# Where a decoder layer's projections wait: banks borrowed from the turned probabilities, self slots rearranged, loads moved

## The chip, the cores and the metric

The kernel runs on one core of one Trainium2 chip. The metric is the device time of the program in microseconds (us), lower is better. A core has TensorE (PE), VectorE (DVE), ScalarE (ACT), GpSimd (POOL) and SyncE (SP), each with its own instruction queue that is worked through in order, and 16 DMA engines shared by all queues. Engines wait for each other by semaphores.

## The reference, cut to what matters

A post-norm decoder layer over x of 8 batches x 256 tokens x 512, with 16 heads of 32:

```python
def _L0_attn_ref(x, Wq, Wk, Wv, Wo):        # 16 query heads, 4 key/value heads
    q = (x @ Wq) ...; k = (x @ Wk) ...; v = (x @ Wv) ...
    att = jnp.where(causal, q @ k.T * scale, -inf)
    return (softmax(att) @ v) @ Wo
def _L0_xattn_ref(q, latent_kv, Wq, Wkv_expand, Wout):   # keys and values from ctx_512 (256 x 128)
    ...causal softmax(q @ Wq.T, latent_kv @ Wkv_expand.T)... @ Wout.T
x = _layernorm(x + _L0_attn_ref(x, ...))
x = _layernorm(x + _L0_xattn_ref(x, ctx_512, ...))
x = _layernorm(x + _L0_ffn_ref(x, ...))      # gates, two levels of entanglement + paths, layer norms
```

Everything is float32. The kernel makes each float32 product from three products of a high and a low part, so an operand is first split: `hi` (a copy into the narrower format, ScalarE) and `lo` (the rest, VectorE or GpSimd).

## The kernel before, in words

**Turns, steps, slots.** The attention phase is a sequence of 17 turns (`Turn`): 8 self turns (one batch each), 8 cross turns, and a flush. `first` is the first, `selfs` a loop of two turns run three times, `last_self` the eighth; then `first_cross`, six `crosses`, `last_cross`, `flush`. A turn has four steps, one for each group of four heads. A step i works in three units: unit 0 is the first 128 queries of four heads, units 1 and 2 the other 128 queries of two heads each. In step i TensorE makes the scores of group i, unit by unit (`scores`, L1225, banks 0 to 2), and between them turns the probabilities of group i-1 (`transposes`, L1237), and behind unit 0 the outputs of group i-2 (`outputs`, L1257 and L1261). After each step stands a slot: projections that fill TensorE while the others work on the scores. The function `fillers` is the list, written by hand: `sk`, `sq`, `sv` are key, query and value projections of self attention, `ck`, `cq`, `cv` of cross attention, `wo` and `wout` the output projections of the turn before, `x1t` transposes of the normed x1, `fu` units of a product of two FFN weights, added up in `acc` (the tensor xb in the profile), `sp` and `gs` splits of FFN weights. Here sk, sq0, sq1 in a turn are for the next batch.

**Banks.** A projection is written to bank 3 or 4 in turn (`P_BANKS`, class `Products`), and waits (`wait_free`) until the product two before it has been drained. The turned probabilities go to banks 5 and 6 in turn (`T_BANKS`), 7 holds the outputs. Three units a step on two banks: unit u of step i has bank (3(i-1)+u) mod 2 of the two.

**Who drains.** ScalarE: exponentials of the step (L920), copies of turned units 0 (self) or 0 and 1 (cross) into probT (L933), then in the slot `hi` of the projections (L855) and copies of sv and cv (L859). VectorE: the maxima (L1049), reciprocals, outputs (L1066, L1070), copies of the other turned units (L1056), then in the slot `lo` (L969), the adds of fused units (L1013), `row_bias` (L998), and for wo the add to xres, statistics, and `normalise` (L1099), which waits for rstd from GpSimd (L769, L771). GpSimd splits outputs (`split_output`), x (`split_x`), FFN rows (L777) and makes path products (`path`, `path_bias`). SP issues all DMAs in order, with its waits between them: `stack` writes a split q or k into three rows (L586, L600), `store` waits for its own store to land, `load_piece` loads a piece of the cross weights, `load_row` FFN rows.

**The cross weights.** They come as pieces of 512 columns, six of them parked in zone_raw. `split_at` says in which slot ScalarE (L847) and VectorE (L961) split them: in `last_self` piece 0 in slot 0, 1 and 2 in slot 1, 3 and 4 ahead of slot 2, 5 ahead of slot 3.

## Time and profile before

| | |
|---|---|
| median of 3 runs | 988.41 us (985.12 to 989.49) |
| the profiled execution: its time, its span | 984.96 us, 983.1 us |
| mean granted clock of TensorE | 0.971 of full speed |
| TensorE matmuls, weight loads | 892.4 us (91%), 735.8 us (75%) |
| VectorE, ScalarE, GpSimd | 677.2 (69%), 550.1 (56%), 496.7 us (51%) |

The attention phase ends near 650 us; behind it stands the FFN phase, which the diff leaves alone. Busy time of matmuls is modelled and they are pipelined; a stretch in which TensorE waits is marked in the timeline as idle, with the engine that ended it. The granted clock is the share of full speed that TensorE was given; its two levels are 1.0 and 0.5 (2.4 and 1.2 GHz), a value between them is a mixture over the stretch.

### The profile page before, as it was taken

How to read it: one execution, taken by the hardware profiler on the slowest of the kernel's cores; microseconds unless marked ns; L12 is line 12 of the kernel's file. 1: busy time of each engine (PE TensorE's matmuls, PEld its weight loads, DVE VectorE, ACT ScalarE, POOL GpSimd, SP SyncE). 2: the span in 40 equal slices, each digit the busy share in tenths (PEclk: the TensorE clock that was granted, in tenths of full speed). 3: DMA queues.
4: the chain of work that ended last, by engine and by line, in shares of the span. 5: the costliest groups of instructions: out<-in, count | busy, mean ns of one | idle time of the engine just before them, and what ended most of it. 6: DMA issues, size and time to landing. Idle time of an engine off the chain costs nothing. (4 is left out here: it accounts for less than half of the span.)

```text
span 983.1 us, 19518 instructions
## 1 busy us (share of the span) xinstructions
PE 892.4 (91%) x5892; PEld 735.8 (75%) x5892; DVE 677.2 (69%) x2055; ACT 550.1 (56%) x1674; POOL 496.7 (51%) x793
## 2 busy tenths in 40 slices
PE   4999999998898899999999998669899999999893
PEld 4888888887776678778777877457678778778672
DVE  4687778786785777777876766426757657667557
ACT  4756556664664566565755556427564464564461
POOL 0445555455755345454645432610665565566466
PEclk9999999999899999999999999879999999999997
DMA  4644243444665556574654636344002001001001
GB/s 155 222 144 158 98 160 128 160 160 143 210 205 145 168 159 194 166 225 121 188 170 138 181 110 197 132 167 155 0 1 85 3 1 55 32 1 40 4 0 43
DMA packets 79075, 118.53 MB, mean 121 GB/s; under 512 B 7920, under 2 KB 41744, under 8 KB 78224
## 3 DMA queue, kind: packets, MB, share of 16 engines
q1 hardware_dynamic: 78992, 117.52, 37.2%
q8 instruction: 40, 0.66, 0.3%
q14 instruction: 43, 0.35, 0.1%
HBM read 58.76 MB, written 17.83 MB: 78 GB/s over the span
## 5 line engine op out<-in xcount | busy, mean ns | idle before, releaser
L920 ACT ACTIVATE prob<-bank,nmax 128x128 f32<-128x128 f32 (+1 forms) x512 | 209.9, 431 | 38.5 <-DVE nmax L1049 36.9
L161 PE MATMUL bank<-w_ffn,hT 128*128 128x512 f32 x768 | 192.8, 402 | 0.0
L1049 DVE CUSTOM_DVE_ANT_0 bank<-bank,mask 128x128 f32<-128x128 f32 (+1 forms) x512 | 167.6, 383 | 4.0 <-PE bank L1225 3.7
L161 PEld LDWEIGHTS bank<-w_ffn,hT 128*128 128x128 f32 x768 | 141.5, 189 | 30.9
L161 PE MATMUL bank<-xT,w_att 128*128 128x256 f32 x864 | 124.1, 298 | 22.0 <-DVE w_att L961 10.3
L161 PEld LDWEIGHTS bank<-xT,w_att 128*128 128x128 f32 x864 | 115.4, 201 | 31.7 <-DVE xT L1037 9.7
L777 POOL TENSOR_TENSOR zone<-raw,zone 128x256 fp32r<-128x256 f32 x128 | 95.2, 776 | 65.8 <-ACT zone L900 65.8
L1237 PE MATMUL bank<-ident,prob 128*128 128x128 f32 x768 | 119.7, 279 | 4.5 <-ACT probT L933 4.4
L933 ACT ACTIVATE probT<-bank 128x512 f32<-128x512 f32 x97 | 58.3, 603 | 92.7 <-PE bank L1261 91.6
L920 ACT ACTIVATION_READ_ACCUMULATOR prob<-bank,nmax 128x1 f32 x512 | 110.0, 215 | 0.0
L1547 ACT ACTIVATE ht<-bank,cols 128x128 f32<-128x128 f32 x192 | 72.3, 457 | 66.0 <-PE bank L1715 66.0
L1225 PE MATMUL bank<-k,q 96*128 96x128 f32 (+1 forms) x512 | 100.2, 299 | 7.3 <-DMA q<-stage 7.3
L161 PE MATMUL bank<-zone 128*128 128x512 f32 x384 | 101.3, 402 | 3.8 <-DVE xb L1013 2.6
L161 PE MATMUL bank<-w_att,oT 128*128 128x512 f32 x384 | 98.8, 407 | 4.7 <-POOL oT L732 4.7
L744 POOL TENSOR_SCALAR rwide<-rden 128x256 f32<-128x256 f32 x64 | 26.0, 407 | 151.0 <-DVE rden L1060 150.7
L1237 PEld LDWEIGHTS bank<-ident,prob 128*128 128x128 f32 x768 | 85.3, 142 | 8.9 <-issue 5.3
L161 PE MATMUL bank<-x2T,zone 128*128 128x512 f32 x384 | 88.5, 391 | 1.6 <-DVE x2T L1569 1.6
L161 PEld LDWEIGHTS bank<-w_att,oT 128*128 128x128 f32 x384 | 72.5, 193 | 21.1 <-issue 4.9
L1454 POOL TENSOR_TENSOR hT<-ht,hT 128x512 fp32r<-128x512 f32 x48 | 69.3, 1445 | 35.8 <-ACT hT L1552 35.8
L1627 DVE TENSOR_TENSOR y<-bank,stage_bias 128x512 f32<-128x512 f32 x64 | 44.1, 690 | 62.0 <-PE bank L161 61.6
L161 PEld LDWEIGHTS bank<-x2T,zone 128*128 128x128 f32 x384 | 72.0, 188 | 17.3 <-issue 2.3
L161 PEld LDWEIGHTS bank<-zone 128*128 128x128 f32 x384 | 68.4, 188 | 18.1 <-DVE xb L1013 3.0
(118 smaller groups left out, 1518.7 us busy)
## 6 DMA issues: line engine op xcount, KB each, us to landing
q<-stage SPq DMA_DIRECT2D x192, 128.0 KB, 2.2
k<-kstage SPq DMA_DIRECT2D x48, 256.0 KB, 3.5
x<-xres SPq DMA_DIRECT2D x16, 512.0 KB, 4.0
raw<-in_ent_wT SPq DMA_DIRECT2D x32, 256.0 KB, 3.8
raw<-in_ent_pw SPq DMA_DIRECT2D x32, 256.0 KB, 4.1
raw<-in_xT SPq DMA_DIRECT2D x8, 512.0 KB, 3.6
raw<-in_path_w SPq DMA_DIRECT2D x8, 512.0 KB, 3.7
xres<-in_x SPq DMA_DIRECT2D x8, 512.0 KB, 4.9
```

Source lines behind the costliest of these rows:

```text
L161: ins = t.matmul(out, lhs(a, k), rhs(b, k), start=first and n == 0 and m == 0, stop=last and n == len(kts) - 1 and m == 2, skip_group_chec ...
L744: g.tensor_scalar(rwide[:, i % 2, :, :].rearrange("p t (j d) -> p t j d", j=HG), src, 1.0, 1.0, ALU.mult, ALU.mult).then_inc(s_wide, 1)
L777: ins = g.tensor_tensor(tiles[:, row % 4, 1, z, c], raw[:, row % RR, z, c], tiles[:, row % 4, 0, z, c].bitcast(F32), ALU.subtract)
L920: ins = s.activation(prob[:, u, c * width:(c + 1) * width], banks[u][:, c * width:(c + 1) * width], ACT.Exp, scale=-1.0, bias=nmax[:, i % ...
L933: s.activation(out, src, ACT.Copy).then_inc(s_cp[u], 1)
L1049: ins = v.tensor_tensor_reduce(scored, scored, mask[:, S - width:S], scale=-1.0, scalar=3e38, op0=ALU.add, op1=ALU.min, accum_out=nmax[:, ...
L1225: ins = t_.matmul(bank[:, c * width:(c + 1) * width], qh[:, j, at:at + P], kh[:, j, 0:width], start=c == 0, stop=c == len(heads) - 1, skip ...
L1237: ins = t_.transpose(bank[:, c * P:(c + 1) * P], prob[:, u, c * P:(c + 1) * P], ident[:, :])
L1454: g.tensor_tensor(hT[:, 1, :, i * P:(i + 1) * P], ht[:, u % HT, :, :], hT[:, 0, :, i * P:(i + 1) * P].bitcast(F32), ALU.subtract).then_inc ...
L1547: ins = s.activation(ht[:, u % HT, c, :], bank[:, c * P:(c + 1) * P], ACT.Identity, bias=shift(u // BT, c), scale=gain(u // BT, c))
L1627: k.drain(("mm", u), v.tensor_tensor(y[:, i, :], banks[plan.bank(("mm", u))][:, :], bias[:, s_, :], ALU.add))
```

## The change

- A third or later projection in a slot: in a slot with three or more products the one at place 1 (place 2 in slot 0 of a self turn) is written to the bank that held turned unit 1, and with more than three the one at place 3 to that of unit 2. It waits for that unit's copy (`s_cp`). The next step's transposes of units 0 and 1 wait (`wait_past`) until what was borrowed has been drained. There are four pairs of semaphores now.
- Self turns: slot 0 is sv0, sv1, sq2; slot 1 sq3, sk0; slot 2 wo0, sq0; slot 3 wo1, sq1. In the last self turn wo0 goes from slot 2 to slot 1, in the first cross turn wo0 and wo1 stand earlier, in the last cross turn cq3, wout0 and wout1 go a slot sooner.
- The next x is loaded from ScalarE's queue at the head of the turn, not from SP's behind slot 0, and GpSimd splits it in slot 0, not 1.
- The copies of sv go from ScalarE to VectorE.
- wo's normalise goes behind the next step (in the last step it stays).
- Pieces 0 and 1 of the cross weights are loaded in the first turn, 2 and 3 at the head of the last self turn, 4 and 5 behind its slot 0; the splits are: piece 0 after slot 0, 1 to 4 after slot 1, 5 after slot 2.

The diff, cut to its core (the replacement of `pr.wait_free(t_, t, name)` by `free(t, name)` in every product, and the counting of four banks, are left out):

```diff
         U, out = ("fu", None), [[], [], [], []]
         if own == "self":
-            out[0] += [("sv", 0), ("sq", 2)]
-            out[1] += [("sv", 1), ("sq", 3)]
+            out[0] += [("sv", 0), ("sv", 1), ("sq", 2)]
+            out[1] += [("sq", 3)]
             if after == "self":
+                out[1 if wo else 2] += [("sk", 0)]
                 if wo:
                     out[2] += [(wo, 0)]
                     out[3] += [(wo, 1)]
-                out[2] += [("sk", 0), ("sq", 0)]
+                out[2] += [("sq", 0)]
                 out[3] += [("sq", 1)]
             else:
-                out[1] += [("x1t", 0), ("x1t", 1)]
-                out[2] += [("wo", 0), ("ck", 0), ("cq", 0), ("sp", 0), ("sp", 1)]
+                out[1] += [("x1t", 0), ("x1t", 1), ("wo", 0)]
+                out[2] += [("ck", 0), ("cq", 0), ("sp", 0), ("sp", 1)]
                 out[3] += [("wo", 1), ("cq", 1), ("ck", 1), ("sp", 2)]
         elif own == "cross" and after:
             out[0] += [U, U, ("cq", 2), U]
             if wo == "wo":
-                out[1] += [U, ("cq", 3), U, ("cv", 0), ("cv", 1), ("x1t", 0), ("x1t", 1), U, ("wo", 0)]
-                out[2] += [U, ("ck", 0), U, ("cq", 0), ("wo", 1)]
+                out[1] += [U, ("cq", 3), U, ("wo", 0), ("cv", 0), ("cv", 1), ("x1t", 0), U, ("x1t", 1)]
+                out[2] += [U, ("wo", 1), ("ck", 0), U, ("cq", 0)]
                 out[3] += [U, U, ("cq", 1), ("ck", 1)]
             else:
                 out[1] += [U, ("cq", 3), U, ("cv", 0), ("cv", 1), ("x1t", 0), ("x1t", 1)]
                 out[2] += [U, ("wout", 0), ("ck", 0), U, ("cq", 0)]
                 out[3] += [U, ("wout", 1), U, ("cq", 1), ("ck", 1)]
         elif own == "cross":
-            out[0] += [("cq", 2)]
-            out[1] += [("cq", 3), ("cv", 0), ("cv", 1), ("gs", 0), ("gs", 1)]
-            out[2] += [("wout", 0), ("gs", 2), ("gs", 3)]
-            out[3] += [("wout", 1), ("gs", 4), ("gs", 5)]
+            out[0] += [("cq", 2), ("cq", 3)]
+            out[1] += [("cv", 0), ("cv", 1), ("wout", 0), ("gs", 0), ("gs", 1)]
+            out[2] += [("wout", 1), ("gs", 2), ("gs", 3)]
+            out[3] += [("gs", 4), ("gs", 5)]
         else:
             out[0] += [("gs", 6), ("gs", 7)]
             out[1] += [("wout", 0), ("wout", 1)]
@@ -280,16 +281,29 @@
         self.units = n - self.unit
         return out[i]
 
+    def borrowed(self, i, j, n):
+
+        if n < 3 or not self.own:
+            return None
+        unit = {2 if self.own == "self" and i == 0 else 1: 1, 3 if n > 3 else -1: 2}.get(j)
+        return None if unit is None else T_BANKS[(UNITS_OF_STEP * (i - 1) + unit) % 2]
+
+    def tile_unit(self, name):
+
+        return next(u for u in (1, 2) if R_BANKS[self.at[name][0]] == T_BANKS[(UNITS_OF_STEP * (self.slot[name] - 1) + u) % 2])
+
     def products(self):
         return [item for i in range(self.steps()) for item in self.fillers(i) if item[0] not in NO_PRODUCT]
 
 
...
+    PARKING = [2, 3, 0, 1, 4, 5]
...
-            return {(0, False): (OUTPUTS, C_KEYS), (1, False): (C_KEYS, C_KEYS + 2), (2, True): (C_KEYS + 2, C_QUERIES),
-                    (3, True): (C_QUERIES, C_VALUES)}.get((i, early), (0, 0))
+            return {(0, False): (OUTPUTS, C_KEYS), (1, False): (C_KEYS, C_QUERIES), (2, False): (C_QUERIES, C_VALUES)}.get((i, early), (0, 0))
...
                 if t is last_self:
-                    load_piece(0)
+                    wait_alone(q, s_wlo, OUTPUTS, s_passed)
+                    load_piece(2)
+                    load_piece(3)
                     q.dma_start(x1b[:, :, :], x1_of[0]).then_inc(s_x1, 16)
...
                 def between(i):
 
-                    if i == 0 and t.after == "self" and t is not first:
-                        wait_alone(q, s_xs, t.lin(1, 1), s_passed)
-                        q.dma_start(xT_raw, xT_of[t.lin(1, 1)]).then_inc(s_xT, 16)
...
                     if i == 2 and t is first:
+                        load_piece(0)
+                        load_piece(1)
...
                     if t is last_self and i == 0:
                         load_path(t)
-                        for n in range(1, 4):
-                            load_piece(n)
+                        wait_alone(q, s_pbm, 2, s_passed)
+                        load_piece(4)
+                        load_piece(5)
                     if t is last_self and i == 1:
                         for l in range(NL):
                             wait_alone(q, s_pbm, 2 * l + 2, s_passed)
                             q.dma_start(A["fd"][l, 1][:, KT, :], acc[:, NP * l, :]).then_inc(s_pbst, 16)
-                        for n in range(4, PARKED):
-                            load_piece(n)
...
+                    if i == (1 if t is first else 0) and t.after == "self":
+                        split_x()
...
-                    if i == 1 and t.after == "self":
-                        split_x()
...
-                elif kind == "sv":
-                    values(t, name, sv[:, t.par, i, :])
...
             def body(t):
+                if t.after == "self" and t is not first:
+                    wait_alone(s, s_xs, t.lin(1, 1), s_passed)
+                    s.dma_start(xT_raw, xT_of[t.lin(1, 1)]).then_inc(s_xT, 16)
...
+                elif kind == "sv":
+                    pr.wait_full(v, t, name)
+                    pr.drain(t, name, v.tensor_copy(sv[:, t.par, i, :], pr.tile(t, name, banks)[:, 0:KV]))
...
+                ready = None
                 for i in range(t.steps()):
                     step(i)
+                    if ready:
+                        normalise(*ready)
+                        ready = None
                     weights(*split_at(t, i, True))
-                    ready = None
                     for name in t.fillers(i):
                         if name[0] in ("wo", "wout"):
                             if ready:
@@ -1109,7 +1146,7 @@
                             ready = add_and_measure(name)
                         elif name[0] != "gs":
                             projection(t, name)
-                    if ready:
+                    if ready and i == t.steps() - 1:
                         normalise(*ready)
                     weights(*split_at(t, i, False))
 
...
+            def free(t, name):
+
+                pr.wait_free(t_, t, name)
+                if t.at[name][0] >= len(P_BANKS):
+                    i = t.slot[name]
+                    if t.before or i > 0:
+                        t_.wait_ge(s_cp[t.tile_unit(name)], t.groups(i - 1))
+
...
                         t_.wait_ge(s_cp[0], t.groups(i))
                     elif t.before or i > 0:
                         t_.wait_ge(s_cp[u + 1], t.groups(i - 1))
+                    if u < 2:
+                        pr.wait_past(t_, t, i + 1, T_BANKS[(U * i + u) % 2])
                     bank = banks[T_BANKS[(U * i + u) % 2]]
```

## Rows read from the trace of the kernel before

**Rows 1.** The page: granted TensorE clock in tenths, 40 slices of 24.6 us.
```profile
PEclk9999999999899999999999999879999999999997
```

**Rows 2.** Windows, turn by turn: length, busy (x) of PE, PEld, DVE, ACT, POOL; clock, DMA.
```profile
170.87:201.16 30.29, 29.28 (x263) 25.75 (x261) 24.06 (x98) 18.32 (x75) 16.24 (x30) 1.00 0.41 143
...
231.32:276.91 45.59, 35.37 (x271) 30.76 (x270) 32.35 (x109) 25.31 (x86) 29.66 (x46) 0.89 0.62 199
276.91:332.28 55.37, 48.30 (x320) 39.30 (x319) 38.02 (x117) 29.42 (x90) 27.56 (x44) 0.94 0.59 168
332.28:376.77 44.49, 42.85 (x306) 34.88 (x305) 32.53 (x110) 27.20 (x88) 20.42 (x35) 1.00 0.57 169
376.77:420.30 43.53, 43.04 (x306) 34.92 (x305) 33.26 (x111) 27.34 (x87) 21.84 (x36) 1.00 0.57 173
```

**Rows 3.** Waits of TensorE, last self turn: total us, times, longest.
```profile
PE bank L161 <- DVE xres L1089: 5.9, 2, 4.0
PE bank L1237 <- ACT probT L933: 3.2, 1, 3.2
```

**Rows 4.** The same from the first cross turn to 343 us.
```profile
PE bank L161 <- DVE xb L1013: 6.5, 3, 3.0
```

**Rows 5.** Windows at the lower clock.
```profile
24.40:27.05 2.65, 2.65 (x13) 2.65 (x13) 0.00 (x0) 1.89 (x9) 0.00 (x0) 0.50 0.03 10
...
244.40:250.40 6.00, 5.95 (x28) 5.98 (x29) 4.58 (x22) 3.72 (x17) 4.16 (x7) 0.51 0.85 316
...
263.20:268.00 4.80, 4.79 (x37) 3.97 (x37) 3.23 (x6) 2.27 (x3) 1.82 (x4) 0.64 0.45 116
...
328.50:332.00 3.50, 3.47 (x17) 3.47 (x18) 1.50 (x3) 1.73 (x4) 2.08 (x4) 0.55 0.03 11
```

**Rows 6.** Timeline of ScalarE and of SP's queue around piece 0.
```profile
243.19 0.63 ACT L847 ACTIVATE w_att<-zone_raw 128x512 fp32r<-128x512 f32 x1 [3.29 <-DMA zone_raw<-in_w_ckv]
...
239.28 0.35 SPq L521 DMA_DIRECT2D zone_raw<-in_w_ckv  x1
```

**Rows 7.** Groups by shape: busy us, mean ns of one, idle before.
```profile
L900 ACT ACTIVATE zone<-raw 128x1024 fp32r<-128x1024 f32 x32 | 34.8, 1090 | 6.5 <-PE bank L161 6.5
...
L969 DVE SCALAR_TENSOR_TENSOR stage<-bank,stage 128x256 fp32r<-128x256 f32 x64 | 27.1, 424 | 65.8 <-ACT stage L855 65.3
...
L855 ACT ACTIVATE stage<-bank 128x256 fp32r<-128x256 f32 x64 | 25.2, 393 | 63.6 <-PE bank L161 63.6
L1066 DVE COPY rT<-bank 128x256 f32<-128x256 f32 x64 | 24.1, 377 | 3.3 <-PE bank L1261 3.2
...
L961 DVE TENSOR_TENSOR w_att<-zone_raw,w_att 128x512 fp32r<-128x512 f32 x16 | 11.8, 772 | 7.1 <-ACT w_att L847 6.8
...
L847 ACT ACTIVATE w_att<-zone_raw 128x512 fp32r<-128x512 f32 x16 | 9.3, 623 | 5.0 <-DMA zone_raw<-in_w_ckv 3.3 <-DMA zone_raw<-in_w_q 1.7
```

**Rows 8.** Timeline of VectorE, first cross turn.
```profile
307.87 0.74 DVE L1099 TENSOR_SCALAR xres<-xres,mv,rstd 128x512 f32<-128x512 f32 x1 [1.11 <-POOL rstd L771]
```

**Rows 9.** Timeline of TensorE, a middle self turn, step 1.
```profile
177.01 0.56 PE L1225 MATMUL bank<-k,q 96*128 96x128 f32 x4
...
178.98 0.86 PE L1257 MATMUL bank<-probT,sv 128*32 128x256 f32 x16 [0.81 <-DVE probT L1056]
```

**Rows 10.** Timeline of VectorE in the same turn.
```profile
173.43 0.55 DVE L1099 TENSOR_SCALAR xres<-xres,mv,rstd 128x512 f32<-128x512 f32 x1 [1.52 <-POOL rstd L771]
...
176.72 0.68 DVE L1056 COPY probT<-bank 128x512 f32<-128x512 f32 x1
...
178.04 0.68 DVE L1056 COPY probT<-bank 128x512 f32<-128x512 f32 x1
```

**Rows 11.** Waits of TensorE, 54 to 120 us (second and third self turn).
```profile
PE bank L161 <- POOL xT L732: 1.5, 1, 1.5
PE bank L1225 <- DMA q<-stage: 1.2, 2, 0.7
```

**Rows 12.** The page: DMA issues, KB each, median us to landing.
```profile
raw<-in_xT SPq DMA_DIRECT2D x8, 512.0 KB, 3.6
```

More of the change, by code:

```diff
@@ L292 @@
 T_BANKS, O_BANK = (5, 6), 7
+R_BANKS = P_BANKS + T_BANKS
 class Products:
@@ L1137, in project_out @@
                 par = 1 - t.par
-                pr.wait_free(t_, t, name)
+                free(t, name)
                 if i == 0:
@@ L1149, in fused @@
                 starts = chunk % (ET // 2) == 0
-                pr.wait_free(t_, t, name)
+                free(t, name)
                 t_.wait_ge(s_flo, row + 2)
```

71 lines of the change are left out of this document (42 added, 29 removed).

## The prediction

> **What bounds the kernel now.** I read the page first. The row of the granted clock [rows 1] is at 9 in all but a few slices: the start, two dips near a third of the span, one at two thirds, the end. TensorE is busy 91% of the span, so time can only come from its idle stretches and from work done at the lower clock. The diff touches only the attention phase (0 to 650 us), so I cut that phase into turns at the first scores of each turn [rows 2]. A middle self turn lasts 30.3 us with 29.3 us busy (four such turns mean 30.3), a steady cross turn 43.5 with 43.0: there the kernel is TensorE-bound, within 1.0 and 0.5 us. The two turns in between are different. The last self turn lasts 45.6 us with 35.4 busy; the first cross turn 55.4 with 48.3, and both have a mean clock below 1. All that is worth having lies there. Then the waits of TensorE in these two turns [rows 3, 4]: 3.2 us for a copy by ScalarE, 5.9 us on the add of xres (a projection wants the bank in which wo lies undrained), 6.5 us on the add into xb, the same thing with the fused units. After three of these idles the work runs at half clock [rows 5]: 6.0, 4.8 and 3.5 us long at 0.51, 0.64 and 0.55; that costs about 2.9 + 1.7 + 1.6 = 6.2 us more, since at 0.51 half of the stretch is loss. So 45.6 + 55.4 hold about 17 us of waits and 6 us of slow work.
>
> **Part 1: new weights sooner.** ScalarE waits 3.3 us for piece 0 of the cross weights and only then copies the turned probabilities: the load is issued at 239.28, at the head of a turn that began at 231.32, because SP first waited out a store [rows 6]. Afterwards pieces 0 and 1 are loaded in the first turn, into room that is free, so this wait (3.2 us on TensorE) and the slow stretch behind it (about 2.9 us) go. The cost moves: four pieces are now split at the end of slot 1 of the last self turn, 4 x 0.62 = 2.5 us on ScalarE and 4 x 0.77 = 3.1 us on VectorE [rows 7], and the fifth one's load stands behind the store wait, sq's stack, the xres load and the path bias. From the turn's start T I place it at T+13, landed at T+18.5 (SP queues about 1 MB of other loads there), VectorE's last split at T+22.6.
>
> **The last self turn worked out.** Its own products need 30.6 us at full clock (29.3 of a middle turn, less sk, plus two x1t, two ck). With VectorE at T+22.6 instead of T+18: cq0 waits 0.1, the transposes of step 3 wait 0.6 for the exponentials, the outputs 1.7 for VectorE's copy of the second unit; then ScalarE has exponentials, two stage copies, two rows of 1.1 us and piece 5 [rows 7] ahead of its copy of unit 0, which costs TensorE 2.7 more. With x1t and ck waiting about 0.5 each and the T0 wait of part 2, that is 30.6 + 7 = 37.5 us. VectorE's own work, 32.4 us in the window [rows 2], allows no less than some 34. So 45.6 - 37.5 = **-8 us**; bounds: -4 if a fourth of the idles and one slow stretch stay on top, -12 at VectorE's floor.
>
> **Part 2: borrowed banks.** Projections so far use two banks in turn, so the third product of a slot waits for the first to be drained, and VectorE drains only after its whole step. Now the second (and fourth) product of a slot with three or more takes a bank of the turned probabilities. In the first cross turn every slot does so. The 6.5 us on xb [rows 4] fall in slots 2 and 3 and in slot 0 of the next turn; the first of them begins because VectorE sat waiting for rstd before normalising (307.87, [rows 8]), which the change defers past the next step, and wo now stands earlier in the slots. A steady cross turn plus one unit (1.45 us) would be 45.0 us, the next turn 43.5: excess 10.4 + 1.0. I take three quarters, since VectorE enters the turn about 2 us late from the last self turn: **-8 us**; bounds -3 and -11.4.
> The price of a borrowed bank is two new waits. A product in unit 1's bank needs that unit's copy (s_cp), and the next step's transposes into that bank need the product drained. In steady cross turns the copy lands 0.2 to 0.3 us after the product before it ends in slots 0 and 1, against 0.2 us of waits removed; the drains come at least 1 us before the transposes. That is **0**, bounds -1.5 and +4 (0.2 us for each of 20 slots).
>
> **Part 3: even self slots.** Before, slot 0 is sv, sq (2.8 us) and step 1 then waits 0.8 us for the copy of unit 2 (177.01 to 178.98, [rows 9]), 0.2 us more in step 2 for sv. After, slot 0 has three products, 4.2 us, and slot 1 sq, sk. The outputs' wait is gone: the copy ends at T+7.9 (178.72 in a turn begun at 170.87 [rows 10]), TensorE comes to it at T+8.3. But sq2 lies in the bank that unit 0 of step 1 uses first. It ends at T+7.6; ScalarE's copy takes 0.39, VectorE's 0.42 [rows 7], each with a semaphore's time before it: drained at T+8.6, when the scores had been over at T+7.9. A wait of 0.7 to 0.9 us stands where one of 0.8 stood. It also needs the copy of unit 1, which ends at T+6.5 in that turn (176.72 + 0.68); VectorE starts about 0.4 us earlier since wo0's normalise no longer precedes step 3, so at T+6.1 against T+6.0. sv's copies go to VectorE, two of under 0.4 us (its 128x256 copy, [rows 7]), 0.25 by size; VectorE waits there anyway. Slot 1 (6.2 us with its step) has VectorE 0.6 us late into step 2, with no one waiting. I get 30.0 us for 30.3: -0.3 x 6 = **-1.8 us**; bounds -5 (all 0.8 to 1.0 gone) and +5 (both waits at 0.9).
>
> **Part 4: x from ScalarE's queue.** The load of the next x went out in SP's queue behind a store's wait and sq2's stack, and its split after slot 1; sk then waited 1.5 us once, q 0.7 and 0.5 us in the second and third turn [rows 11]. Now ScalarE issues it first thing in the turn (0.4 to 1.0 us of issuing into an idle of 1.6 before its copy), GpSimd splits it in slot 0 by T+10.5, sk wants it at T+13.2. GpSimd's rwide behind it is ready at T+11.3, wanted at T+16. sq2's stack on SP has 5.6 us before it is needed instead of 3.8. So **-2.8 us**; bounds 0 and -2.8. The queue's place is what I count; the Trainium skill, DMA: Bandwidth & Descriptors, section Issuing engines are not separate DMA queues, says the same from the other side: another issuing engine saves issue time only. If a second queue also shortened the landing of 3.6 us [rows 12], nothing more would come, as nobody would wait for it.
>
> **The first turn pays.** Its clock is at 0.50 until about 28.5 [rows 5]. sv1 moves into that stretch (2.5 us instead of 1.5), sq2 ends 1.5 us later, and step 2, which already waits 0.65 for q, goes with it: **+1.6 us**; bounds 0 and +3. In the last cross turn cq3 moves to slot 0 and ends the waits for its bank (2.4) and for q (1.7), but xres and the gate loads go out 1.9 us later behind its stack, VectorE then stands before wout's add, and the end hangs on GpSimd's gate splits as before: **0**, bounds +-2.
>
> **Sum.** -8 - 8 + 0 - 1.8 - 2.8 + 1.6 + 0 = -19.0. The profiled execution took 984.96 us (span 983.1); 984.96 - 19 = 966. The median of the three runs is 988.41, 3.45 above it, so 969.5; I say 970.
>
> **Rivals.**
> (a) The stalls of the transition only change their name: the split of four pieces in one place holds VectorE, ScalarE's rows hold unit 0's copy, and the drop of the clock returns. Speaks for it: VectorE is busy 32.4 of 45.6 us, and I have already 4.3 us of new idles in step 3. Each drop costs 1.6 to 2.9. Then parts 1 and 2 give -3 and -4: 988.4 - 10 = 978.
> (b) The loads don't come in time: piece 4 and xres land late (5 us each from issue, behind one another), SP's queue moves every stack, and the change does nothing in the transition. Only parts 3 and 4 less the first turn stay, -3: 985, within 0.5%.
> (c) The other side: the waits for drained borrowed banks. If a drain comes 1.6 us after the product instead of 1.0, each self turn loses 0.6 more (8 x 0.6 = 5), and from 0.9 us per slot in the 24 cross slots (+22) it outweighs the 16 of the transition: 988.4 - 19 + 5 + 22 = 996. Against it: the drains' slack of 1 us in the cross slots.
> (d) The new 0.8 us idles in front of unit 0's transposes drop the clock in the self turns. From rows 5 a drop costs up to 2.9 us; seven of them are +20, so 990. Against it: the present idles of 0.6 to 0.8 us per turn left the clock at 1.00 in five turns (one of them is in [rows 2]). The Trainium skill, TensorE: Matmul & The Clock Gate, section A second HAM failure mode: psum-queue depth-cycling, tells of a kernel in which cycling through banks brought small idles that made the clock swing; by that rule 990, and this trace, which cycles four banks already at 1.00, doesn't bear it out.
>
> **Chances and range.** Forecast 0.60, (a) 0.25, (b) 0.08, (c) 0.04, (d) 0.03. The summed bounds of the large terms, taken as independent, give +-6 to 8 round 970; with (a) the range is 960 to 982, and holds 8 in 10. A change under 0.5% (5 us) can't be told from none here. Faster by more: 0.60 + 0.25 + a little of (b) = 0.86; within: 0.08; slower: 0.06.
>
> **What would show it.** Right: the last self turn near 37.5 us, the first cross turn near 47, no ScalarE wait on w_ckv; a wait of 0.7 to 0.9 us of the transposes (L1237's line) on VectorE's stage in step 1 of each self turn, in place of the one on probT; self turns near 30.0. Wrong: self turns over 30.6; waits on ScalarE's or VectorE's w_att over 5 us in the last self turn; clock dips in both turns; cross turns over 44.

## The result and the profile after

The changed kernel takes 972.07 us (median of 4 runs, 971.42 to 972.83), the kernel before, run beside it, 986.76 us (4 runs, 984.89 to 989.49). The ratio is 0.985 with a 95% interval of 0.982 to 0.987: 1.5% shorter, clear of the noise, within the range and 2 us above the forecast. The profiled execution took 972.83 us, its span is 971.0 us at a mean clock of 0.970.

The row of the granted clock, which answers [rows 1]: the 8 in the eleventh slice (246 to 270 us) is gone, and the second slice (24 to 49 us) reads 7.

```profile
PEclk9799999999999999999999999879999999999997
```

The windows turn by turn, which answer [rows 2] (first turn, a middle self turn, the last self turn, the first cross turn and the three after it; last cross turn with the flush). Columns as there.

```profile
21.51:51.32 29.81, 26.48 (x188) 24.86 (x189) 19.33 (x86) 18.34 (x75) 10.16 (x19) 0.77 0.57 185
173.99:204.44 30.45, 29.53 (x263) 25.84 (x262) 24.76 (x100) 17.61 (x73) 16.40 (x31) 1.00 0.44 142
234.74:275.27 40.53, 32.94 (x270) 28.18 (x269) 31.90 (x110) 24.74 (x84) 30.34 (x45) 0.96 0.60 190
275.27:323.92 48.65, 45.27 (x320) 36.93 (x319) 37.56 (x118) 29.38 (x90) 27.04 (x44) 1.00 0.73 208
323.92:367.86 43.94, 42.28 (x307) 34.79 (x306) 33.55 (x111) 27.10 (x88) 22.24 (x38) 1.00 0.55 172
367.86:410.85 42.99, 42.47 (x307) 34.81 (x306) 33.33 (x111) 27.18 (x87) 21.53 (x36) 1.00 0.59 176
410.85:454.65 43.80, 42.88 (x315) 35.89 (x314) 33.03 (x110) 26.01 (x86) 22.47 (x38) 1.00 0.62 190
583.26:638.02 54.76, 35.69 (x280) 27.94 (x279) 28.93 (x107) 25.68 (x88) 23.46 (x45) 0.89 0.45 152
```

The reader is to see that the last self turn went from 45.6 to 40.5 us and the first cross turn from 55.4 to 48.7, now at clock 1.00; that a cross turn with nothing special in it also got shorter (43.5 to 43.0, 44.6 to 43.8); that a middle self turn did not (30.29 to 30.45); and that the first turn got longer, at a clock of 0.77.

Middle self turns, timeline of TensorE, which answers [rows 9]:

```profile
180.48 1.68 PE L161 MATMUL bank<-xT,w_att 128*128 128x256 f32 x12 [0.33 <-DVE probT L1090]
...
183.15 0.66 PE L1284 MATMUL bank<-ident,prob 128*128 128x128 f32 x4 [0.59 <-DVE stage L1000]
183.74 0.86 PE L1304 MATMUL bank<-probT,sv 128*32 128x256 f32 x16
```

The wait of 0.81 us for the copy of unit 2 is gone, and two new ones stand in its place: 0.33 us of sq2 for the copy of unit 1 (in every second turn) and 0.59 us of the next transposes for the drain of sq2.

The last self turn, timeline of TensorE, and SP's queue, which answer [rows 3, 6]:

```profile
250.46 1.86 PE L1240 MATMUL bank<-ident,x1b 128*128 128x128 f32 x8 [2.09 <-DMA x1b<-x]
251.97 3.97 PE L161 MATMUL bank<-w_att,oT 128*128 128x512 f32 x12
...
261.29 0.95 PE L161 MATMUL bank<-ctxT,w_att 128*128 128x256 f32 x6 [1.85 <-issue]
...
268.95 0.63 PE L1284 MATMUL bank<-ident,prob 128*128 128x128 f32 x4 [1.81 <-ACT probT L964]
...
243.35 0.83 SPq L548 DMA_DIRECT2D zone_raw<-in_w_cq  x2
244.23 0.43 SPq L652 DMA_DIRECT2D x1b<-x  x1
```

ScalarE's wait for piece 0 and the 5.9 us on xres are gone (a wait of ScalarE of 1.0 us for a later piece is new). What is left begins with 2.1 us for the load of x1b, which SP issued at 244.23 behind pieces 2 and 3. The eight transposes and twelve products behind it took 1.86 and 3.97 us. There follow 1.9 us marked "issue" ahead of ck0, which had to wait for GpSimd's split of ctx (it ended at 261.18), and 1.8 us for ScalarE's copy of unit 0 in step 3.

### The profile page after: what moved, and what is told of

The parts are those of the page before. It is cut to its first block and busy times, and to the rows that moved or that the text cites. A ratio compares the mean times of both kernels' runs of the same rounds, so it can differ in the third digit from the quotient of the medians.

```text
span 971.0 us, 19561 instructions
## 1 busy us (share of the span) xinstructions
PE 890.4 (92%) x5892; PEld 735.9 (76%) x5892; DVE 682.1 (70%) x2071; ACT 544.1 (56%) x1658; POOL 499.1 (51%) x793
## 5 line engine op out<-in xcount | busy, mean ns | idle before, releaser
L161 PE MATMUL bank<-xT,w_att 128*128 128x256 f32 x864 | 120.1, 292 | 12.5 <-DVE w_att L992 11.0
```

Source lines behind the costliest of these rows:

```text
L161: ins = t.matmul(out, lhs(a, k), rhs(b, k), start=first and n == 0 and m == 0, stop=last and n == len(kts) - 1 and m == 2, skip_group_chec ...
```

## Where each run stands, turn by turn

The lengths are differences between the starts of the turns' first scores in each run's timeline (us). "Middle" is the mean of the fourth to seventh turn, "cross" the mean of the five steady cross turns, "rest" runs from the start of the last cross turn to the end of the span. The time is the median of each kernel's runs, with that of the kernel before, run beside it.

```
                           time / before  turn 1     2     3  middle last self 1st cross  next  cross   rest
before                                      25.7  31.4  32.3  30.26    45.6      55.4     44.5  43.86  387.0
after                      972.1 / 986.8    29.8  31.6  30.3  30.38    40.5      48.7     43.9  43.08  387.7
after again                972.2 / 985.5    29.1  31.6  30.3  30.38    40.9      48.5     43.9  43.09  388.0
no borrowing               989.5 / 985.6    30.9  31.2  32.2  31.64    40.9      54.0     44.4  43.81  387.9
old self slots             967.2 / 985.6    28.1  31.7  30.1  29.89    38.8      47.4     44.0  43.17  388.5
x from SP                  986.5 / 985.6    31.0  32.3  32.3  33.52    38.9      48.8     44.0  43.22  390.4
old pieces                 974.6 / 985.6    31.8  31.6  30.3  30.39    43.2      47.6     43.9  43.26  387.6
x1b first                  970.6 / 987.4    30.7  31.5  30.3  30.38    36.9      47.8     44.0  43.26  390.1
ctx first                  973.8 / 987.4    29.8  32.7  30.3  30.39    40.9      49.1     44.0  43.13  389.8
sq first                   970.5 / 987.4    29.0  31.5  30.5  30.63    38.6      47.8     44.0  43.14  392.0
late pieces                973.3 / 987.4    30.9  31.6  30.3  30.39    38.8      49.4     44.0  43.16  390.6
borrowing alone            977.7 / 985.5    26.5  30.8  30.1  30.11    42.5      55.4     43.5  43.21  391.1
old self slots, x1b first  966.6 / 985.5    29.6  31.1  30.1  29.87    38.2      47.8     44.0  43.28  391.7
the same, old place of x   967.4 / 985.5    28.2  31.8  31.1  29.92    37.4      48.2     44.0  43.16  388.0
```

The changed kernel was run a second time as a control:

> The changed kernel once more, unedited, to see how far one kernel moves from one chip call and one profile to the next: 971 to 973 by both theories, the middle self turns at 30.3 to 30.5 us, and the first turn and the last self turn, where the clock moves, within 1.5 us of the first profile.

It took 972.23 us (6 runs, 970.15 to 977.67). The middle and cross turns repeat within 0.02 us on the mean; turn 1 and the last self turn within 0.7, the first turn's start (21.5 and 19.1) only within 2.4. The runs "old self slots", "x from SP" and "late pieces", whose last self turn is the same code, show 38.8 to 38.9 there, "ctx first" 40.9: a single profile decides 2 us in that turn and not less. The rest varies from 387.6 to 392.0 without any edit to it. The expectation held in each of its points.

## Experiments

**Borrowing taken out.** `borrowed` answers None; everything else is the changed kernel.

```diff
-        if n < 3 or not self.own:
+        if True:
             return None
```

> Leaves out the borrowing alone: every projection lies in bank 3 or 4 again, the new orders of the slots, the loads and the deferred normalise stay. Theory A (the borrowed banks carry the gain of the cross turns): the waits of the projections for the drain of xb and xres come back in the first cross turn and its neighbour (4 to 6 us), the steady cross turns are 0.5 to 0.8 us longer each (3 to 5 us in seven), in the self turns slot 0's sq2 waits for sv0's drain by VectorE, which comes only after its step, while the 0.6 us wait of the transposes goes: 0 to +1 us each. Sum +8 to +14 us: 980 to 986. Rival B (reordering and the deferred normalise did it): within 3 us of the changed kernel, 970 to 975.

989.51 us (12 runs), 1.005 of the kernel before (1.003 to 1.008): 17 us over the changed kernel. Windows of the first cross turn and of a middle self turn, and the waits of TensorE in the two:

```profile
282.36:336.35 53.99, 48.63 (x321) 39.70 (x320) 37.70 (x117) 29.19 (x90) 28.01 (x45) 0.94 0.66 187
...
147.52:179.76 32.24, 30.65 (x262) 27.25 (x261) 24.80 (x100) 17.72 (x73) 16.46 (x30) 0.95 0.39 134
...
PE bank L161 <- DVE sv L1015: 1.6, 1, 1.6
...
PE bank L161 <- DVE xb L1047: 2.1, 1, 2.1
PE bank L161 <- DVE xres L1123: 2.0, 1, 2.0
```

Theory A, and stronger than it said. The first cross turn has the waits on xb and xres again and the clock of 0.94; each steady cross turn is 0.7 us longer, as before the change. What I had not expected: the even self slots can't live without the borrowed bank. sq2 then waits 1.6 us for the copy of sv0, and in two of the four middle turns the clock is at 0.95; these two are 2.0 us longer than in the changed kernel, the two that keep 1.00 0.5 us, 1.3 us on the mean. Leaving these self turns out, borrowing is worth 5.3 + 0.5 + 5 x 0.73 = 9.5 us.

**Borrowing alone.** The kernel before with the banks, and nothing else of the change: old slots, loads, splits, ScalarE's copies of sv, the normalise at the slot's end.

```diff
+    def borrowed(self, i, j, n):
+        if n < 3 or not self.own:
+            return None
...
+                    if u < 2:
+                        pr.wait_past(t_, t, i + 1, T_BANKS[(U * i + u) % 2])
```

> The kernel before with the borrowed banks alone: its own orders of the slots, its loads, its splits, its copies of sv by ScalarE and its normalise at the slot's end; only the third and later product of a slot of three or more (place 1, and 3 with more than three) borrows, which in a middle self turn is sk in slot 2. Theory A (borrowing is what pays, and needs none of the rest; leaving it out of the changed kernel gave all of the gain back): the steady cross turns 0.6 us shorter each (-4), the first cross turn and its neighbour 4 to 6 us shorter, the middle self turns 0.2 to 0.4 us shorter; the last self turn stays near 44 to 46: 985.5 to 987 less 10 to 13 = 973 to 976. Rival B (the borrowed bank needs the new orders and the deferred normalise, since with the old ones the drain comes no sooner): 981 to 986.

977.69 us (8 runs), 0.993 of before (0.990 to 0.996): 8 of some 15 us. It is between the two. The cross turns gained as A said (43.2 for 43.9), the middle turns a little less (0.15 us each); the first cross turn gained nothing at all (55.4), as B said. Neither had the last self turn right: it is 42.5 us for 45.6, the 5.9 us on xres gone and 3.5 us for VectorE's split of the weights in their place. Timeline of that turn, VectorE, ScalarE, TensorE:

```profile
299.17 0.69 DVE L1118 TENSOR_TENSOR xres<-bank,xres 128x512 f32<-128x512 f32 x1 [1.41 <-PE bank L161]
...
302.03 0.74 DVE L1128 TENSOR_SCALAR xres<-xres,mv,rstd 128x512 f32<-128x512 f32 x1 [1.11 <-POOL rstd L798]
...
303.87 0.37 ACT L949 ACTIVATE prob<-bank,nmax 128x128 f32<-128x128 f32 x1 [2.03 <-DVE nmax L1078]
...
305.25 0.61 ACT L962 ACTIVATE probT<-bank 128x512 f32<-128x512 f32 x1
...
306.01 0.94 PE L161 MATMUL bank<-ctxT,w_att 128*128 128x256 f32 x6 [2.00 <-ACT probT L962]
```

Read it as a chain. wo0 lies last in slot 1, so VectorE adds it only at 299.17, when step 2 has already begun (298.97), takes the statistics, waits 1.11 us for rstd and normalises at 302.03. Only then come the maxima, so ScalarE's exponentials start at 303.87, and its copy of unit 1, which stands behind them, at 305.25. ck0 lies in that unit's bank: TensorE waits 2.0 us at 306.01, and 3.0 us in the next slot, where ScalarE's exponentials stand 3.0 us for the maxima again (the profile names no releaser for that wait of TensorE). The wait for a drain ([rows 4, 8]) has become a wait for a copy. wo's earlier place and the deferred normalise should take this chain apart. The rest of the change without the banks gives 54.0, the banks without the rest 55.4, both together 48.7. Of the rest, the old pieces (47.6) and, with x1b first, the old self slots and the old place of x (48.2) cost this turn nothing; what is left are wo's place and the deferred normalise. No run takes these two apart, and the move of sv's copies wasn't tried by itself either.

**Old self slots.** First seven turns as sv0 sq2 | sv1 sq3 | wo0 sk sq0 | wo1 sq1.

```diff
-            out[0] += [("sv", 0), ("sv", 1), ("sq", 2)]
-            out[1] += [("sq", 3)]
+            if after == "self":
+                out[0] += [("sv", 0), ("sq", 2)]
+                out[1] += [("sv", 1), ("sq", 3)]
...
-                out[2] += [("sq", 0)]
+                out[2] += [("sk", 0), ("sq", 0)]
```

> Slots of the self turns as before the change (sv0 sq2 | sv1 sq3 | wo0 sk sq0 | wo1 sq1) in the first seven turns; the last self turn as changed. In the first six of them nothing is borrowed but in slot 2 (three products). Theory A (evening the slots is worth nothing, as the wait for the borrowed bank took the place of the wait for unit 2's copy, and it costs the first turn its slow start): the first turn is 2 to 4 us shorter, the middle turns within 0.2 us of 30.4: 968 to 970.5. Rival B (evening is worth the 0.8 to 1 us a turn that the waits of before came to, and only the first turn pays): six turns of +0.8 less 3: 973 to 976.

967.17 us (5 runs), ratio 0.983 (0.980 to 0.986): theory A, though not as it said. The first turn is 28.1 us for 29.8 and 29.1, less than the 2 to 4 us expected. The middle turns, which were to stay within 0.2 us of 30.4, take 29.9 us, half a microsecond less than the changed ones and 0.4 less than before. All the waits of TensorE in two middle turns:

```profile
PE bank L1307 <- DVE probT L1093: 1.1, 2, 0.8
```

The old wait for the copy of unit 2 stays (0.8 and 0.3), the two new ones are absent, and sk in slot 2 has its borrowed bank.

**sq first in slot 0.** The borrowed product is then sv1, with a single copy to drain it.

```diff
-            out[0] += [("sv", 0), ("sv", 1), ("sq", 2)]
+            out[0] += [("sq", 2), ("sv", 0), ("sv", 1)]
```

> Slot 0 of the self turns is sq2, sv0, sv1 in place of sv0, sv1, sq2: the borrowed product is then sv1, which one copy drains, in place of sq2, which ScalarE's and VectorE's copies drain one after the other. Theory A: the wait of the next step's transposes for the borrowed bank (0.6 us in each self turn) goes or is halved: -2 to -4 us in seven or eight turns, 968 to 970. Rival B: VectorE drains three products in a row at the slot's end either way, the last of them at the same time, and the outputs wait for its copies instead: within 1 us of 972.

970.48 us (5 runs, 970.24 to 973.08). Waits in two middle turns:

```profile
PE bank L1284 <- DVE sv L1015: 1.9, 2, 1.0
PE bank L161 <- DVE probT L1090: 0.2, 1, 0.2
```

The mechanism is B's: the wait grew to 1.0 us a turn and has sv's copy in the place of sq2's. VectorE comes to the slot's drains only after its step, so what counts is its last drain, not how many copies the borrowed product needs. The middle turns are 0.25 us longer. The median is 1.6 us lower all the same, which these turns don't explain; turn 1 and the last self turn were shorter in the profile, whose own time was 973.1.

**x from SP's queue again**, at the head of the turn, with the split in slot 0 kept.

```diff
+                if t.after == "self" and t is not first:
+                    wait_alone(q, s_xs, t.lin(1, 1), s_passed)
+                    q.dma_start(xT_raw, xT_of[t.lin(1, 1)]).then_inc(s_xT, 16)
                 if t is last_self:
```

> The next x is loaded by SP, as the first thing between the turns and behind SP's waits there, in place of ScalarE's queue at the head of the turn; GpSimd still splits it in slot 0. Theory A (what counts is the place in the queue: SP stands there in the wait for a store that ends some 12 us into the turn): GpSimd waits for x with its split, the key projection waits for GpSimd, 1 to 4 us in each of six turns: +6 to +24 us, 978 to 996. Rival B (the load has slack enough wherever it is issued, and the gain of the early turns came from the slots): within 2 us of 972.

986.48 us (12 runs), 0.999 of before (0.997 to 1.002): theory A, +14 us. The window of a middle turn that begins at 149.48, then SP's queue, GpSimd and TensorE in it:

```profile
149.48:183.27 33.79, 31.43 (x262) 27.27 (x261) 24.87 (x100) 17.72 (x73) 16.37 (x31) 0.95 0.37 128
...
153.55 0.40 SPq L602 DMA_DIRECT2D x<-xres  x1
156.78 0.41 SPq L650 DMA_DIRECT2D raw<-in_xT  x1
...
160.27 1.51 POOL L758 TENSOR_SCALAR xT<-raw 128x256 fp32r<-128x256 f32 x4 [4.65 <-DMA raw<-in_xT]
...
164.78 2.46 PE L161 MATMUL bank<-xT,w_att 128*128 128x256 f32 x12 [1.74 <-POOL xT L762]
```

SP issues a store at 153.55 and stands until it has landed; x goes out at 156.78, T+7.3 (not T+12, as the expectation had it). In the changed kernel ScalarE issues it at 174.80, T+0.8. GpSimd waits 4.7 us with its split, sk waits 1.7 us for GpSimd, and the products behind it take 2.46 us instead of 1.5: clock 0.95, 3.1 us a turn. The Trainium skill, DMA: Bandwidth & Descriptors, section Issuing engines are not separate DMA queues, states that another issuing engine saves issue time only. The trace agrees: from issue to landing x took 4.0 us out of ScalarE's queue in the changed kernel (median of six), and 3.5 us after SP's issue here GpSimd had it. But an engine that waits between its DMAs makes its place worth 6.5 us of lateness here.

**Old slots and old place of x together**, beside the old slots with x from ScalarE (both with x1b first, below).

```diff
+                    if i == 0 and t.after == "self" and t is not first:
+                        wait_alone(q, s_xs, t.lin(1, 1), s_passed)
+                        q.dma_start(xT_raw, xT_of[t.lin(1, 1)]).then_inc(s_xT, 16)
...
+                    if i == 1 and t.after == "self":
+                        split_x()
```

> The changed kernel with the self slots of before in the first seven turns and the load of x1b ahead of pieces 2 and 3. Theory A (the two act in different turns and add up: -0.5 us in each middle turn and -1 in the first, and 2 to 3.5 us of the last self turn): 964.5 to 966.5. Rival B (they share a cause in the last self turn, which in the run with the old slots alone was already 1.7 us shorter): 967 to 968.

> The same with the next x loaded by SP behind slot 0 and split by GpSimd after slot 1, both as before the change. Theory A (with sk back in slot 2 the middle turns have room for the old place, and the new place only spares the second and third turn their 2.8 us of waits): 2 to 3 us longer than the kernel with the old slots and x1b first, near 968. Rival B (x from ScalarE's queue is worth as much as in the changed kernel, where the load by SP cost 15 us): over 975. Rival C (worth nothing with these slots): within 1 us.

966.58 us (6 runs, 965.84 to 970.22) and 967.35 us (6 runs, 964.47 to 972.35). With the old slots the new place of x is worth 1.0 us in turn 3, nothing in the middle turns, and nothing that the medians tell from zero: rival C, or a little of A. (The 0.7 us in turn 2 don't count: "old self slots", with x from ScalarE, has 31.7 there too.) So moving x early is no gain in itself; it is what the even slots need, whose sk stands a slot sooner. Of the first run's own two theories the last self turn speaks for B: with the old slots x1b first takes it from 38.8 to 38.2 only (37.4 with the old place of x). TensorE's 2.0 us for x1b are gone, but it now stands 3.8 us for ScalarE's copies where it stood 1.0. The median, 0.6 us under that of the old slots alone, says the same.

**Old pieces.** Loads and splits of the cross weights as before the change; x1b is then issued right behind piece 0.

```diff
-            return {(0, False): (OUTPUTS, C_KEYS), (1, False): (C_KEYS, C_QUERIES), (2, False): (C_QUERIES, C_VALUES)}.get((i, early), (0, 0))
+            return {(0, False): (OUTPUTS, C_KEYS), (1, False): (C_KEYS, C_KEYS + 2), (2, True): (C_KEYS + 2, C_QUERIES),
+                    (3, True): (C_QUERIES, C_VALUES)}.get((i, early), (0, 0))
```

> Loads and splits of the cross weights' pieces as before the change (piece 0 at the head of the last self turn, split in slot 0, 1 and 2 in slot 1, 3 and 4 ahead of slot 2, 5 ahead of slot 3), all else changed. Theory A (the late first piece made the 3.2 us wait and the slow stretch behind it): the last self turn is 4 to 7 us longer, with ScalarE waiting some 3 us for the piece, and the first turn 0 to 1 us shorter: 975 to 979. Rival B (the new order of the projections and the borrowed bank in that turn did it; the wait for the piece is covered by other waits): within 2 us of 972.

974.55 us (6 runs), 2.5 us over the changed kernel and just under A's 975; the last self turn is 43.2 us, 2.7 longer where A said 4 to 7, and the first turn is not shorter. ScalarE's wait for piece 0, TensorE's wait for the copy behind it, and the longest wait of TensorE in that turn with the clock after it:

```profile
246.89 0.63 ACT L872 ACTIVATE w_att<-zone_raw 128x512 fp32r<-128x512 f32 x1 [2.21 <-DMA zone_raw<-in_w_ckv]
...
248.15 0.63 PE L1282 MATMUL bank<-ident,prob 128*128 128x128 f32 x4 [0.17 <-ACT probT L962]
...
266.89 2.93 PE L161 MATMUL bank<-xT,w_att 128*128 128x256 f32 x12 [5.16 <-DVE w_att L990]
...
268.00:276.00 8.00, 8.00 (x54) 6.45 (x54) 5.51 (x22) 4.91 (x15) 4.68 (x7) 0.69 0.63 180
```

So the mechanism isn't A's. The late piece costs ScalarE 2.2 us, but TensorE only 0.17, where it was 3.16 before. With three products in slot 0 TensorE comes to that copy 11.6 us into the turn, not 10.0, and the piece is split at T+10.6, not T+11.9. As B had it, the new order covers this wait. What the old pieces cost is 5.2 us in slot 2, where the first query projection stands until VectorE, behind the whole of step 2, has split pieces 3 and 4, and then work at 0.69 from 268 to 276 us (about 2.5 us, estimated from that window). The new splits, a slot sooner, take this away.

**x1b first.** Its load goes ahead of pieces 2 and 3.

```diff
+                    q.dma_start(x1b[:, :, :], x1_of[0]).then_inc(s_x1, 16)
                     wait_alone(q, s_wlo, OUTPUTS, s_passed)
                     load_piece(2)
                     load_piece(3)
-                    q.dma_start(x1b[:, :, :], x1_of[0]).then_inc(s_x1, 16)
```

> In the last self turn the load of x1b (the rows that x1t turns) is issued ahead of pieces 2 and 3 instead of behind them and behind the wait for the weights' split. Theory A (the 2.1 us wait of x1t for this load is real path): the last self turn is 1 to 2.1 us shorter: 970 to 971. Rival B (the load is late because SP stands in the store's wait before either, so the order behind it moves it by under a microsecond, or the wait moves to the next stage): 971.5 to 973.

970.63 us (5 runs, 968.63 to 972.36). Window of the last self turn, and TensorE where the wait was:

```profile
235.36:272.29 36.93, 31.44 (x270) 26.78 (x269) 31.84 (x110) 24.41 (x84) 30.40 (x45) 1.00 0.65 208
...
248.82 1.04 PE L1240 MATMUL bank<-ident,x1b 128*128 128x128 f32 x8
249.91 3.03 PE L161 MATMUL bank<-w_att,oT 128*128 128x512 f32 x12
```

SP issued the load at 243.58, 0.6 us sooner against the turn's start. The wait is gone, the same transposes and products take 1.04 and 3.03 us instead of 1.86 and 3.97, and the clock is 1.00 throughout. The turn is 36.9 us for 40.5: 2.1 of waiting and 1.8 of slow work. In this profile the gain is more than theory A asked; the median, 970.6, is in A's range. The 3.6 us are at the high end: against the three runs with 38.8 to 38.9 us it is 2 us, and with the old slots 0.6 (38.8 to 38.2). And against "old pieces", where x1b is early too, the new pieces are worth 43.2 - 36.9 = 6.3 us in the profiles and 3.9 us in the medians.

**ctx first.** GpSimd splits ctx ahead of wo0's rstd.

```diff
+                    if i == 1 and t is last_self:
+                        split_ctx()
                     for name in t.fillers(i):
```

> In slot 1 of the last self turn GpSimd splits ctx before it takes the rstd of wo0 instead of behind it, so ck0 has its operand about 2.5 us sooner. Theory A: the 1.85 us in which TensorE stands before ck0 go, and the normalise that rstd feeds has slack since it is deferred: 970 to 971. Rival B: rstd then comes late, VectorE stands in the deferred normalise ahead of the weights' split, and the time is given back within the turn: 972 to 974.

973.77 us (5 runs): rival B. GpSimd, then TensorE, in the last self turn:

```profile
252.26 0.40 POOL L755 TENSOR_SCALAR ctxT<-ctx_raw 128x256 fp32r<-128x256 f32 x1
...
258.56 0.46 POOL L796 TENSOR_SCALAR rstd<-mv 128x1 f32<-128x1 f32 x1 [5.08 <-DVE mv L1130]
...
263.51 0.63 PE L1272 MATMUL bank<-k,q 96*128 96x128 f32 x4 [1.01 <-ACT prob L953]
...
265.47 0.86 PE L1306 MATMUL bank<-probT,sv 128*32 128x256 f32 x16 [0.85 <-DVE probT L1092]
```

The split is ready at 253.5 and the 1.9 us ahead of ck0 are gone. But nothing behind it came sooner: rstd still stands until wo0's statistics are there at 258.5, and step 3 now waits 1.0 us for ScalarE's probabilities and 0.85 for VectorE's copy. The turn is 40.9 us, as the control's. That points to VectorE (31.9 us busy of 40.9) as what sets this half of the turn; no run shows it by itself.

**Late pieces.** Pieces 0 and 1 behind slot 3 of the first turn.

```diff
-                    if i == 2 and t is first:
+                    if i == 3 and t is first:
                         load_piece(0)
                         load_piece(1)
```

> In the first turn pieces 0 and 1 are loaded behind slot 3 instead of slot 2. Theory A (the two loads of 256 KB stand ahead of q0's and q1's rows for the next turn, or share the DMA engines with them, and so make the 3.05 us wait of the second turn for q<-stage and the slow clock behind it): 1 to 3 us shorter, 969 to 971. Rival B (q0 was issued before the pieces; the wait comes from the slot's later end, behind the slow start): within 1 us of 972.

973.30 us (6 runs, 971.02 to 977.31), turn 1 at 30.9 us: rival B. The two loads aren't what makes the first turn longer, nor the wait for q at its end, which is 4.1 us here; nor are they in "old pieces", where there are none and turn 1 takes 31.8.

## Why the prediction was right, and where its terms were not

The forecast was 970 for 972.1, but by errors that partly cancel: the change was 14.7 us of the 19.0 forecast, and the median of the kernel before was itself 1.65 us lower with its fourth run than the 988.41 that the forecast started from. Against the two profiled spans (-12.1 us) the terms came out as follows; the medians moved by -14.7, since the profiled execution of before was 1.8 us under its median and that of after 0.8 over.

| term | predicted | measured | |
|---|---|---|---|
| last self turn | -8 | -5.1 | x1b |
| first cross turn and the next | -8 | -6.7 and -0.6 | as said |
| steady cross turns | 0 | -3.9 | missed |
| middle self turns (4) | -0.3 each | +0.12 each | wrong sign |
| turns 2 and 3 | -2.8, and -0.3 each | +0.1 and -2.0 | |
| start and first turn | +1.6 | +0.7 and +4.1 | too small |
| last cross turn to the end | 0 | +0.7 | as said |

(The prediction also read two dips near a third of the span off the page; the page has one 8, at 246 to 270 us, and the slow stretches come from [rows 5]. Its three quarters of 11.4 us are 8.6, not 8.)

**Last self turn.** That new weights sooner pay was right, but not why. Part 1 counted 3.2 us of TensorE's wait for the copy and 2.9 us of slow work behind it, 6.1 in all, and the two profiles "old pieces" and "x1b first" are 6.3 us apart; that the numbers agree is luck. In "old pieces" that wait is 0.17 us, covered by the even slot 0, and what the late pieces cost is the wait of 5.2 us for VectorE's split of pieces 3 and 4 and the slow stretch behind it. The term that failed in size is "x1t and ck waiting about 0.5 each": they waited 2.1 and 1.9, and the first drew a slow stretch after it. I had listed what piece 5 stands behind on SP, but not x1b, which the same edit puts behind a wait and two loads. Without that wait the turn takes 36.9 us in its profile, for 37.5 worked out. The 2.7 us ahead of unit 0's transposes came as 1.8, the 1.7 for the outputs as 0.5.

**First cross turn.** Nearly right in size and right in place (48.7 us for about 47), and shown to need both the banks and the rest of the change; that it is the deferred normalise with wo's earlier place follows by elimination.

**Steady cross turns.** I counted 0.2 us of waits there and called the price 0. The rows of the matmuls show 3.1 us of waits in the five turns before and 2.8 after; most of the gain is in the rows of the weight loads. Their waits in the five steady cross turns, before, and the same after (two rows of 4.0 and 3.4 us that are the same in both are left out):

```profile
PEld bank L161 <- DVE xb L1013: 5.3, 9, 1.1
...
PEld bank L161 <- DVE kstage L969: 2.2, 4, 0.8
PEld bank L1195 <- ACT cv L859: 1.7, 5, 0.5
PEld bank L161 <- DVE xres L1089: 1.4, 5, 0.3
PEld bank L1195 <- issue: 1.4, 3, 0.5
PEld bank L161 <- DVE stage L969: 1.3, 2, 0.9
```

```profile
PEld bank L161 <- issue: 8.0, 18, 1.1
...
PEld bank L1240 <- ACT cv L886: 2.5, 5, 0.5
```

The rows shown sum to 13.3 us before and 10.5 after: 2.8 us less. The busy time of the matmuls fell with the turn, 43.04 to 42.47 in turns that hold the same products, and five times 0.57 is 2.85 us: it looks as if what a late weight load cost had been booked as busy matmuls. Without borrowing the weight loads' waits sum to 13.2 us, the matmuls are at 43.04 again and the turn at 43.56; with borrowing alone they are 10.9 us and 42.50. That borrowing gives this gain is shown by both its runs; which of the short waits counted is not.

**Middle self turns.** The exchange of waits was forecast at the right places and sizes (0.7 to 0.9 at the transposes, measured 0.6 to 0.7). What was left out is that the copy of unit 1 is late as well (0.33, "T+6.1 against T+6.0"), and that the old slots with a borrowed bank for sk are better than either kernel: 29.9 us. Term -1.8, measured about +0.5 in the four; the even slots cost 0.5 us in each turn against the old ones.

**Turns 2 and 3.** Part 4 gave them its 2.8 us, and the waits of [rows 11] for q and xT are indeed gone between 54 and 120 us; what is left there are the new 1.3 us for the drain of sq2 (two waits) and 0.4 for probT. Turn 2 kept its old length because its first half was still slow (clock 0.89 from 51 to 67 us, 0.95 over the turn); turn 3 lost its 2.0. But borrowing alone, with x in the old place, has 30.1 us in turn 3 too, so I can't claim that x's new queue did it. By itself it is worth the 1.0 us of the last pair of runs at most.

**First turn.** The clock from 28 to 36 us, before and after:

```profile
28.00:36.00 8.00, 7.35 (x70) 6.57 (x69) 5.64 (x31) 4.55 (x20) 4.92 (x10) 0.97 0.72 225
```

```profile
28.00:36.00 8.00, 7.72 (x38) 7.56 (x39) 4.28 (x21) 3.37 (x15) 2.74 (x7) 0.53 0.25 56
```

The direction was right, but the bound of +3 was not, and the reason (sv1 moves into the slow stretch) is not shown. In this profile the stretch did not end at 28.5 but near 35.5, so step 1 and slot 1 ran slow as well and step 3 begins 2.5 us later in the turn; the turn's end waits 3.05 us for q in the place of 1.43. But "ctx first", whose first turn is the same code, hardly has the slow stretch:

```profile
28.00:36.00 8.00, 7.29 (x66) 6.40 (x65) 5.32 (x28) 4.48 (x19) 4.66 (x9) 0.94 0.47 152
```

Its step 3 begins only 0.5 us later in the turn than before, and the turn still takes 29.8 us, since it ends with 4.9 us of waiting for q. SP issued q's rows at 43.29, and the next turn's scores began 7.1 us after that; before it was 42.88 and 3.6 us. With the old slots the clock is at 1.00 from 28 to 36, and the turn takes 28.1 to 29.6, with 3.6 to 5.2 us for q at its end. So the loss has two parts, the slow stretch (2.5 us in the first profile, 0.5 in this one) and the late q (1.6 and 3.5), and only the first was forecast. What makes q late stays open: it is not the two pieces. The runs of this turn scatter by more than 1 us.

**The rivals.** (a) was half true: stalls did change their name in the last self turn, and one drop of the clock came back, at a price of up to 3.6 us with the wait before it, not 9. (b) fell, though its mechanism, a load behind SP's wait, is just what hit x1b and what "x from SP" shows at full size (+14). (c) did not occur in the cross turns; in the self turns it is the 0.6 us that the old slots don't have. (d) fell: with waits of 0.6 to 0.7 us the middle turns stay at 1.00. A lower clock came with longer waits in two experiments: 1.6 us (no borrowing) and 1.7 us (x from SP), both 0.95 of the turn. The Trainium skill, TensorE: Matmul & The Clock Gate, section A second HAM failure mode: psum-queue depth-cycling, ties the swinging clock to small idles that come with cycling through banks. Here the number of banks alone doesn't decide: the changed kernel, with more of them, and the kernel before, with two for its projections, both hold 1.00 in these turns, and "no borrowing", with two, drops in two of the four.

Of the signs named beforehand, no wait of ScalarE on w_ckv, cross turns under 44 us and middle turns under 30.6 came; the new wait of the transposes came at 0.6 to 0.7 us for 0.7 to 0.9; the last self turn (40.5 for 37.5) did not.

**The best version** measured is the changed kernel with its old self slots, with or without x1b first: 967.2 and 966.6 us, 5 us under the changed kernel and 1.7 to 1.9% under before. These two, and the one with the old place of x (967.4), can't be told apart by their medians.

## What to carry to other kernels

When a load or a product moves, list all that the same edit puts behind a wait on that queue, not only what it moves on purpose; in the profiles x1b took back up to 3.6 us of the 6.3 that the new pieces gave. When a run gives the size that was forecast, look whether it is the forecast wait that went: here it was another one. A third accumulator bank is worth something only if what frees it is not queued behind the work that it was to decouple: look where the drain and the copy stand in their engines' order. Where matmuls fill a stretch to 99%, read the waits of the weight loads too.

## What the runs showed of the hardware

Waits of TensorE of 0.6 to 0.8 us left the granted clock of a turn at 1.00. A wait of 2.1 us (x1b) was followed by a stretch at 0.69 (250.46 to 255.94) that cost 1.8 us more, nearly its own length again; waits of 1.6 and 1.7 us went with turns at 0.95. But length alone doesn't decide: without borrowing the same wait of 1.6 us stands in a turn at 0.95 (147.52 to 179.76) and in one at 1.00 (210.78 to 241.50), and "x1b first" has waits of 1.6 and 2.0 us in a turn at 1.00. What does decide is open. In the first turn the window from 28 to 36 us stood at 0.97 before and at 0.53 after, but at 0.94 in "ctx first" with the same code, so the order of the products doesn't decide it by itself. For the same products in a cross turn the busy time of the matmuls was 43.04 us with 13.3 us of waits of the weight loads in five turns, and 42.47 us with 10.5.
